# Cross-attention with a gate: score columns laid beside the gate weight, softmax per tile, output shared out over three engines

## The chip, the core and the metric

The kernel runs on one core of one Trainium2 chip. The metric is the device time of one execution in microseconds (us). Before the change it is 416.56 us, the median of three runs. The engines named below are TensorE (PE; its weight loads are listed apart as PEld), VectorE (DVE), ScalarE (ACT), GpSimd (POOL) and SyncE (SP), which here only issues transfers. Each engine runs its own list of instructions in the order written, and engines meet through semaphores: `wait_ge` holds the engine, and all that is written behind it, until a count is reached.

## What is computed

16 batches, 512 queries and 77 keys each, width 512. Cut to what matters, the reference is:

```python
qp = q @ Wq + bq
kp = k @ Wk + bk
vp = v @ Wv + bv
w = jnp.einsum('bqd,bkd->bqk', qp, kp) * scale
w = jax.nn.softmax(w, axis=-1)
x = jnp.einsum('bqk,bkd->bqd', w, vp)
gate = jnp.concatenate((qp, x), axis=-1) @ Wg + bg
x = x * mask[..., None]
x = x * jax.nn.sigmoid(gate)
return x + q0
```

`q0` is the input `q`; keys and values are the same context rows. The mask is one number per row.

## The kernel before

**Precision.** Each product is made of three: an operand is split into a high part (a rounded copy, made by ScalarE) and a low part (what is left, made by VectorE or GpSimd), and high x high, high x low and low x high are summed. So a product over the width of 512 is 4 chunks x 3 = 12 matmuls.

**First stage** (to about 119 us of the trace). Weights are folded: `mt` holds for every batch the 78 key columns (77 and one of zeros) already multiplied by both projections, so that scores are `x @ mt`; `wqg` is the query half of the gate weight multiplied by the query projection; `v_ext` holds per key the value row and beside it that row times the value half of the gate weight. A list of jobs passes through PSUM banks; `v_st` tiles go to memory and come back as `v_ext`.

**Second stage, the loop over 16 batches.** A batch has 4 tiles of 128 queries, numbered n = 4b + t over all batches. `xT` is x turned, with a high and a low part, in two buffers that alternate by batch; its raw form `x_raw` has one buffer. TensorE runs, per batch:

- `gate_main` (L422 to L431): 12 matmuls of 512 columns a tile, `xT` against `wqg`, into one of three banks;
- `turn_probs` (L442): 4 transposes of the probabilities of the whole batch;
- `attend` (L453 to L461): 4 matmuls of 512 columns a tile: two add the value part of the gate to the tile's gate bank, two make the attention output;
- `scores_T` (by the helper at L323): 12 matmuls of 512 columns for the *next* batch, with keys as rows, and `turn_scores` (L401), 4 transposes of them.

ScalarE makes the high part of the next batch's `xT` (L493, four chunks, right at the start of a batch), copies the turned probabilities (L573, L575), and makes the tanh of each tile (L587) and one exp a batch (L497). VectorE does the softmax once a batch in wide instructions (L627 to L634, L724 to L732), the low part of the probabilities (L736) and two instructions a tile: `product` (L744) and `output` (L755), which multiplies by the mask and adds the rows of x. GpSimd makes the low part of `xT` (L781), four chunks in a row, a batch ahead. SyncE's queue loads `x_raw` two batches ahead as soon as it is free, loads the rows and stores the output.

The order around the change is written out by hand, per engine:

```python
for b in range(B):
    more = b + 1 < B
    gate_main(b, 0)
    gate_main(b, 1, range(0, 1))
    turn_probs(b)
    gate_main(b, 1, range(1, C))
    attend(b, 0)
    gate_main(b, 2)
    attend(b, 1)
    if more:
        scores_T(b + 1)
```

## Time and profile before

| | us |
|---|---|
| median of 3 runs (416.47 to 417.1) | 416.56 |
| the profiled execution | 416.89 |
| its span, first to last instruction | 415.1 |
| TensorE busy in it | 407.6 |
| VectorE busy | 228.9 |
| ScalarE busy | 144.7 |
| GpSimd busy | 124.0 |

The span is 1.8 us shorter than the execution's own time. The loop over batches begins at 119.35 us. TensorE matmuls overlap in the records: the length of one is about 0.39 us, while the next one starts 0.23 us after it. So the pace is read from starts, not from lengths.

### The profile page before, as it was taken

The page shows a single profiled execution, that of the slowest core. Times are in us where ns is not written, and L with a number is a line of the kernel's source. Part 1 is how long each engine was busy: PE and PEld are TensorE (multiplying, and loading weights), DVE is VectorE, ACT ScalarE, POOL GpSimd, SP SyncE. Part 2 cuts the span into 40 slices and gives each one's busy share as a digit, 9 for nine tenths or more (in the row PEclk, how much of TensorE's full clock was granted, in tenths as well). Part 3 has the DMA queues.
Part 4 walks back from the last instruction along what each step waited for, and adds up shares of the span by engine and source line. Part 5 has one row for each costly group of instructions (what it writes and reads, how often), then busy time and mean ns, then how long its engine had stood idle before and what let it go on. Part 6 is the DMA issues. An engine that isn't in the chain of part 4 may idle for free.

```text
span 415.1 us, 5234 instructions
## 1 busy us (share of the span) xinstructions
PE 407.6 (98%) x1874; PEld 325.5 (78%) x1874; DVE 228.9 (55%) x404; ACT 144.7 (35%) x251; POOL 124.0 (30%) x96
## 2 busy tenths in 40 slices
PE   8999999999999999999999999999999999999995
PEld 4889986888776878787787878778787877878784
DVE  3687557554563646547364554736455564645554
ACT  5644242325223414233241414424241432324121
POOL 0005125445635405052340505133150504325000
PEclk9999999999999999999999999999999999999999
DMA  7993542568699795866859576786958677595412
GB/s 267 384 415 130 148 130 109 203 200 292 206 305 269 255 304 171 253 196 226 261 189 286 191 252 204 230 221 214 280 199 263 190 242 225 205 275 199 132 53 101
DMA packets 42934, 92.11 MB, mean 222 GB/s; under 512 B 4780, under 2 KB 4780, under 8 KB 42268
## 3 DMA queue, kind: packets, MB, share of 16 engines
q1 hardware_dynamic: 41756, 89.68, 66.4%
q10 hardware_dynamic: 1152, 2.10, 1.6%
q8 instruction: 15, 0.25, 0.3%
q14 instruction: 11, 0.09, 0.1%
HBM read 64.75 MB, written 27.00 MB: 221 GB/s over the span
## 4 chain that ended last, share of the span: by engine, by line
PE 93%; POOL 2%; ACT 2%; DMA 1%; DVE 1%; issue 0%; DVEq 0%
PE bank L430 42%; PE bank L323 32%; PE bank L454 3%; PE bank L461 3%; PE bank L460 3%; PE bank L453 3%; PE bank L346 3%; PE bank L442 2%; POOL xT L781 1%; PE bank L401 1%; DMA wkT_raw<-in_wkT 1%; PE bank L383 1%; POOL wg L781 1%; ACT vT L488 0%; ACT wg L484 0%
## 5 line engine op out<-in xcount | busy, mean ns | idle before, releaser
L430 PE MATMUL bank<-wqg,xT 128*128 128x512 f32 x768 | 192.4, 396 | 0.0
L430 PEld LDWEIGHTS bank<-wqg,xT 128*128 128x128 f32 x768 | 142.1, 188 | 30.6
L781 POOL TENSOR_TENSOR xT<-x_raw,xT 128x512 fp32r<-128x512 f32 x64 | 87.5, 1397 | 178.7 <-ACT xT L493 178.7
L744 DVE SCALAR_TENSOR_TENSOR prod_sb<-tanh_sb,bank 128x512 f32<-128x512 f32 x64 | 43.9, 686 | 72.2 <-ACT tanh_sb L587 72.2
L587 ACT ACTIVATE tanh_sb<-bank 128x512 f32<-128x512 f32 x64 | 38.3, 598 | 125.0 <-PE bank L454 124.3
L755 DVE SCALAR_TENSOR_TENSOR out_sb<-prod_sb,half_mask,x_rows 128x512 f32<-128x512 f32 x64 | 54.5, 851 | 1.7
L323 PE MATMUL bank<-xT,mt 128*77 128x512 f32 x192 | 47.1, 394 | 0.8 <-POOL xT L781 0.8
L323 PEld LDWEIGHTS bank<-xT,mt 128*77 128x77 f32 x192 | 27.8, 146 | 16.9 <-POOL xT L781 1.3
L493 ACT ACTIVATE xT<-x_raw 128x512 fp32r<-128x512 f32 x64 | 35.3, 622 | 0.4 <-DMA x_raw<-in_xT 0.4
L323 PE MATMUL bank<-wv,ctxT 128*128 128x512 f32 (+1 forms) x120 | 30.2, 401 | 0.0
L323 PE MATMUL bank<-wg,vT 128*128 128x512 f32 (+1 forms) x120 | 29.7, 394 | 0.4 <-DVE vT L612 0.3
L736 DVE TENSOR_TENSOR wT<-bank,wT 77x512 fp32r<-77x512 f32 x16 | 11.0, 686 | 30.5 <-ACT wT L573 30.5
L323 PE MATMUL bank<-ctxT,g_s 128*128 128x416 f32 x144 | 27.5, 351 | 0.0
L323 PEld LDWEIGHTS bank<-ctxT,g_s 128*128 128x128 f32 x144 | 26.9, 188 | 0.4
L323 PEld LDWEIGHTS bank<-wg,vT 128*128 128x128 f32 (+1 forms) x120 | 21.9, 185 | 6.4 <-DVE vT L612 0.7
L461 PE MATMUL bank<-v_ext,wT 122*128 122x512 f32 x64 | 25.5, 398 | 0.0
L460 PE MATMUL bank<-v_ext,wT 128*128 128x512 f32 x64 | 25.5, 398 | 0.0
L454 PE MATMUL bank<-v_ext,wT 122*128 122x512 f32 x64 | 25.3, 395 | 0.0
L323 PEld LDWEIGHTS bank<-wv,ctxT 128*128 128x128 f32 (+1 forms) x120 | 21.6, 186 | 4.6
L453 PE MATMUL bank<-v_ext,wT 128*128 128x512 f32 x64 | 25.0, 391 | 0.0
L781 POOL TENSOR_TENSOR v_st<-v_f,v_st 128x512 fp32r<-128x512 f32 (+1 forms) x10 | 13.2, 1316 | 31.4 <-ACT v_st L484 31.4
L627 DVE TENSOR_SCALAR sT<-bank,sb_c 77x512 f32<-77x512 f32 x16 | 11.9, 746 | 18.8 <-PE bank L323 18.8
(73 smaller groups left out, 354.2 us busy)
## 6 DMA issues: line engine op xcount, KB each, us to landing
x_rows<-in_x SPq DMA_DIRECT2D x32, 512.0 KB, 6.9
out_y<-out_sb SPq DMA_DIRECT2D x64, 256.0 KB, 4.3
x_raw<-in_xT SPq DMA_DIRECT2D x60, 256.0 KB, 10.4
v_ext<-v_dram SPq DMA_DIRECT2D x32, 308.0 KB
v_dram<-v_st SPq DMA_DIRECT2D x18, 512.0 KB, 3.3
v_ext<-v_dram SPq DMA_DIRECT2D x16, 180.0 KB
ctxT_raw<-in_ctxT SPq DMA_DIRECT2D x4, 624.0 KB, 10.6
ctx_rows<-in_ctx SPq DMA_DIRECT2D x4, 616.0 KB
```

The source lines that it names most:

```text
L323: last = pe.matmul(ps, lhs(s, c), rhs(m, c), start=(c == 0 and n == 0), stop=(c == C - 1 and n == 2))
L346: last = pe.matmul(bank[bank_of(J["g", cc])][:, :], wkT[:, s, c, cc * P:(cc + 1) * P], wqT[:, m, c, :], start=(c == 0 and n == 0), stop=(c ...
L430: pe.matmul(gate_ps[n % 3][:, :], xT[b % 2][:, s, c, q], wqg[:, m, c, :], start=(c == 0 and (s, m) == PRODUCTS[0]), stop=False)
L453: pe.matmul(ps[:, :], wT[:, 0, q], v[:, 0, D:2 * D], start=False, stop=False)
L454: pe.matmul(ps[:, :], wT[0:K_B, 1, q], v[0:K_B, 1, D:2 * D], start=False, stop=True).then_inc(gate_done, 1)
L460: pe.matmul(ps[:, :], wT[:, 0, q], v[:, 0, 0:D], start=True, stop=False)
L461: pe.matmul(ps[:, :], wT[0:K_B, 1, q], v[0:K_B, 1, 0:D], start=False, stop=True).then_inc(attn_done, 1)
L493: act.activation(xT[b % 2][:, HI, c], x_raw[:, c], ACT.Copy).then_inc(xT_hi, 1)
L587: act.activation(tanh_sb[:, n % 2, :], gate_ps[n % 3][:, :], ACT.Tanh, scale=0.5).then_inc(tanh_made, 1)
L744: dve.scalar_tensor_tensor(prod_sb[:, n % 2, :], tanh_sb[:, n % 2, :], 1.0, attn_ps[n % 2][:, :], ALU.add, ALU.mult).then_inc(prod_made, 1)
L755: dve.scalar_tensor_tensor(out_sb[:, t, :], prod_sb[:, n % 2, :], half_mask[:, n:n + 1], x_rows[b % 2][:, t, :], ALU.mult, ALU.add).then_i ...
L781: pool.tensor_tensor(dst, src, f32(hi_), ALU.subtract).then_inc(made, 1)
```

## The change

The 78 score columns of a batch are laid beside the gate weight in a tile `ws` (two buffers, alternating by batch): two halves, each with 39 score columns, one column of zeros and 256 columns of the gate weight, 296 in all (`HN`). `main` multiplies a tile of x by both halves at once: 24 matmuls of 296 columns a tile, into two PSUM banks. They stand in place of `gate_main`'s 12 of 512 and of `scores_T`'s and `turn_scores`' share. Scores then have queries as rows from the start, and the softmax is done for each tile.

- **ScalarE** copies the gate part out of PSUM (`x_part`), makes the exp with its row sum for a tile, applies the mask (`mask`), makes one chunk of the next batch's `xT` in each tile, and makes the tanh, now from SBUF.
- **VectorE** adds the bias row to the scores, takes maximum, reciprocal and the probabilities for each tile; `gate` adds the value part of the gate, which now has its own PSUM bank, to the copy; `product` stays; `output` goes.
- **GpSimd** adds the rows of x (`output`), copies the score columns of a batch into `ws` (`place_mt`), fills the second `ws` once, and makes one chunk of the low part of `xT` in each tile.
- **SyncE** sends the scores' bias through memory and back as a row for all partitions (`sb_row`).

Core of the diff:

```diff
+            def main(n, chunks):
+                b, q = n // T, slice(n % T * P, (n % T + 1) * P)
+                ps = main_ps[n % 2]
+                if chunks[0] == 0:
+                    pe.wait_ge(xT_lo, (b + 1) * C)
+                    pe.wait_ge(mt_placed, b + 1)
...
+                        pe.wait_ge(gx_made, n - 1)
+                for c in chunks:
+                    for s, m in PRODUCTS:
+                        for h in range(2):
+                            last = pe.matmul(ps[:, h, 0:HN], xT[b % 2][:, s, c, q], ws[b % 2][:, m, c, h, :],
+                                             start=(c == 0 and (s, m) == PRODUCTS[0]), stop=(c == C - 1 and (s, m) == PRODUCTS[2]))
...
+            for n in range(NT + 2):
+                if 0 < n < NT:
+                    main(n, range(0, C // 2))
+                if n >= 2:
+                    attend(n - 2)
+                if n < NT:
+                    main(n, range(C // 2, C - 1))
+                if 1 <= n <= NT:
+                    turn_probs(n - 1)
+                if n < NT:
+                    main(n, range(C - 1, C))
...
+            def x_part(n):
+                act.wait_ge(main_done, n + 1)
+                act.wait_ge(sc_made, n + 1)
...
+                act.activation(gx[:, n % 3, :].rearrange("p (h n) -> p h n", h=2), main_ps[n % 2][:, :, HK + 1:HN], ACT.Copy).then_inc(gx_made, 1)
...
+            for n in range(1, NT + 2):
+                if n <= NT:
+                    x_part(n - 1)
+                    exps(n - 1)
+                if n >= 3:
+                    mask(n - 3)
+                b, c = (n - 1) // T + 1, (n - 1) % T
+                if b < B:
+                    act.wait_ge(main_done, (b - 1) * T)
+                    act.wait_ge(xT_in[c], 16 * (b + 1))
+                    act.activation(xT[b % 2][:, HI, c], x_raw[:, c], ACT.Copy).then_inc(xT_hi, 1)
+                if n >= 2:
+                    tanh_tile(n - 2)
+                if n <= NT:
+                    high_probs(n - 1)
...
+            for n in range(1, NT + 2):
+                if n <= NT:
+                    softmax_max(n - 1)
+                    softmax_rest(n - 1)
+                if n >= 2:
+                    gate(n - 2)
+                if n <= NT:
+                    low_probs(n - 1)
+                if n >= 2:
+                    product(n - 2)
...
+            for n in range(1, NT + 2):
+                b, c = (n - 1) // T + 1, (n - 1) % T
+                if b < B:
+                    xT_lo_of(b, (c,))
+                if c == 0 and 2 <= b < B:
+                    place_mt(b)
+                if n >= 3:
+                    output(n - 3)
```

**TensorE, last tile of batch 0 and first of batch 1.** `psum` is now one tensor of eight banks; `ws_58` and `xT_71` are batch 1's buffers. Before, the same place reads (L442 is `turn_probs` of batch 1):

```order
L430 MATMUL bank<-wqg,xT_68 128x512 x6
L453 MATMUL bank<-v_ext_60,wT 128x512
L454 MATMUL bank<-v_ext_60,wT 128x512
L460 MATMUL bank<-v_ext_60,wT 128x512
L461 MATMUL bank<-v_ext_60,wT 128x512
L430 MATMUL bank<-wqg,xT_69 128x512 x15
L442 MATMUL bank<-ident,prob 128x128 x4
```

and now, with the waits:

```order
L418 MATMUL psum<-ws_57,xT_70 128x296 x6
L430 MATMUL psum<-ident,prob 128x128 [waits wT_lo,prob_made]
L418 MATMUL psum<-ws_57,xT_70 128x296 x6
L418 MATMUL psum<-ws_58,xT_71 128x296 [waits gx_made,mt_placed,xT_lo]
L418 MATMUL psum<-ws_58,xT_71 128x296 x11
L444 MATMUL psum<-v_ext_61,wT 128x512 [waits pre_made,wT_lo,wT_dup]
```

The first matmul of a batch now waits for `xT_lo`, all four chunks of that batch's low part, and `turn_probs` stands in every tile instead of once a batch.

**ScalarE, the same place.** Before, the four chunks of batch 1's `xT` stand together, ahead of all tanh instructions of batch 0:

```order
L493 ACTIVATE xT_69<-x_raw 128x512 [waits xT_in0]
L493 ACTIVATE xT_69<-x_raw 128x512 [waits xT_in1]
L493 ACTIVATE xT_69<-x_raw 128x512 [waits xT_in2]
L493 ACTIVATE xT_69<-x_raw 128x512 [waits xT_in3]
L587 ACTIVATE tanh_sb<-bank 128x512 [waits v_stored1,vg_stored0,vg_stored1,v_stored0,gate_done] x2
```

and now the last chunk of batch 1 stands behind the copy of tile 3's result, which waits for `main_done` of that tile:

```order
L565 ACTIVATE gx<-psum 128x512 [waits tanh_made,sc_made,main_done]
L571 ACTIVATE expd,rowsum<-sc,negmax 128x78 [waits prob_made,negmax_made]
L603 ACTIVATE out_sb<-prod_sb,half_mask 128x512 [waits prod_made]
L615 ACTIVATE xT_71<-x_raw 128x512 [waits xT_in3,main_done]
L594 ACTIVATE tanh_sb<-gx 128x512 [waits prod_made,pre_made]
L581 ACTIVATE wT<-psum 128x128 [waits wT_zeroed,turned]
L583 ACTIVATE wT<-wT 32x128 [waits wT_hi]
```

What moved is the place of the conversion: from a batch ahead to the end of the tile just before its use.

**VectorE, one tile of the loop.** Before, the two instructions of a tile, twice:

```order
L744 SCALAR_TENSOR_TENSOR prod_sb<-tanh_sb,bank 128x512 [waits attn_done,tanh_made]
L755 SCALAR_TENSOR_TENSOR out_sb<-prod_sb,half_mask,x_rows_89 128x512 [waits half_made,x_in00,prod_made]
L744 SCALAR_TENSOR_TENSOR prod_sb<-tanh_sb,bank 128x512 [waits attn_done,tanh_made]
L755 SCALAR_TENSOR_TENSOR out_sb<-prod_sb,half_mask,x_rows_89 128x512 [waits x_in00,prod_made]
L627 TENSOR_SCALAR sT<-bank,sb_c 77x512 [waits sT_done]
```

and now, one tile:

```order
L734 TENSOR_TENSOR sc<-psum,sb_row 128x78 [waits exp_made,main_done]
L736 TENSOR_REDUCE rowmax<-sc 128x1 [waits sc_made]
L738 TENSOR_SCALAR negmax<-rowmax 128x1 [waits max_made]
L743 RECIPROCAL rinv<-rowsum 128x1 [waits exp_made]
L748 TENSOR_SCALAR prob<-expd,rinv 128x77 [waits turned,rinv_made]
L748 TENSOR_SCALAR prob<-expd,rinv 128x19
L748 TENSOR_SCALAR prob<-expd,rinv 128x32
L758 TENSOR_TENSOR gx<-psum,gx 128x512 [waits gx_made,vgate_done]
L753 TENSOR_TENSOR wT<-psum,wT 77x128 [waits wT_hi]
L765 SCALAR_TENSOR_TENSOR prod_sb<-tanh_sb,psum 128x512 [waits attn_done,tanh_made]
```

The wide softmax of four tiles is now ten narrow and wide instructions in each tile, with a wait at nearly every one.

## Rows read from the trace of the kernel before

**Rows 1.** The page: busy time by engine, and the chain that ended last.
```profile
PE 407.6 (98%) x1874; PEld 325.5 (78%) x1874; DVE 228.9 (55%) x404; ACT 144.7 (35%) x251; POOL 124.0 (30%) x96
...
PE 93%; POOL 2%; ACT 2%; DMA 1%; DVE 1%; issue 0%; DVEq 0%
```

**Rows 2.** Timeline of TensorE, one batch: start, length in us, line, operation, tiles, count.
```profile
197.47 0.60 PE L442 MATMUL bank<-ident,prob 128*128 128x128 f32 x4
...
199.99 0.39 PE L453 MATMUL bank<-v_ext,wT 128*128 128x512 f32 x1
...
200.93 2.94 PE L430 MATMUL bank<-wqg,xT 128*128 128x512 f32 x12
...
215.81 0.60 PE L442 MATMUL bank<-ident,prob 128*128 128x128 f32 x4
```

**Rows 3.** Timeline: shorter matmuls, two weight loads in a row, the first matmuls.
```profile
44.71 2.61 PE L323 MATMUL bank<-ctxT,g_s 128*128 128x416 f32 x13
...
6.22 0.30 PEld L346 LDWEIGHTS bank<-wqT,wkT 128*128 128x128 f32 x2 [1.49 <-ACT wkT L484]
...
1.19 4.44 PE L337 MATMUL bank<-zeros 128*128 128x512 bf16 x10 [1.19 <-DVE zeros L644]
```

**Rows 4.** Groups by line and form (busy us, mean ns, idle before); last two: minimum/median/maximum ns.
```profile
L781 POOL TENSOR_TENSOR xT<-x_raw,xT 128x512 fp32r<-128x512 f32 x64 | 87.5, 1397 | 178.7 <-ACT xT L493 178.7
...
L744 DVE SCALAR_TENSOR_TENSOR prod_sb<-tanh_sb,bank 128x512 f32<-128x512 f32 x64 | 43.9, 686 | 72.2 <-ACT tanh_sb L587 72.2
L587 ACT ACTIVATE tanh_sb<-bank 128x512 f32<-128x512 f32 x64 | 38.3, 598 | 125.0 <-PE bank L454 124.3 <-DMA v_dram<-v_st 0.8
L493 ACT ACTIVATE xT<-x_raw 128x512 fp32r<-128x512 f32 x64 | 35.3, 622 | 0.4 <-DMA x_raw<-in_xT 0.4
...
L573 ACT ACTIVATE wT<-bank 128x512 fp32r<-128x512 f32 x16 | 9.6, 599 | 29.1 <-PE bank L442 29.1
...
L724 DVE TENSOR_REDUCE rowsum<-expd 128x4 f32<-128x308 f32 x16 | 7.5, 467 | 0.0
L497 ACT ACTIVATE expd<-shifted 128x308 f32<-128x308 f32 x16 | 7.4, 463 | 42.4 <-DVE shifted L634 42.4
...
L726 DVE RECIPROCAL rinv<-rowsum 128x4 f32<-128x4 f32 x16 | 2.9, 178 | 0.5
...
L685 DVE TENSOR_SCALAR half_mask<-mask_c 128x64 f32<-128x64 f32 x1 | 0.2, 188 | 0.0
...
L731 DVE TENSOR_TENSOR prob<-expd,rinv x16: 229/230/1324, 121.4 to 396.1; 128x76 f32<-128x76 f32 x16
L732 DVE TENSOR_TENSOR prob<-expd,rinv x16: 278/284/285, 122.6 to 396.2; 128x128 f32<-128x128 f32 x16
```

**Rows 5.** Timeline: hops from engine to engine, ScalarE to GpSimd among them.
```profile
124.93 2.19 ACT L493 ACTIVATE xT<-x_raw 128x512 fp32r<-128x512 f32 x4
...
125.64 5.48 POOL L781 TENSOR_TENSOR xT<-x_raw,xT 128x512 fp32r<-128x512 f32 x4 [3.06 <-ACT xT L493]
```

**Rows 6.** VectorE's output instruction alone: minimum/median/maximum ns.
```profile
L755 DVE SCALAR_TENSOR_TENSOR out_sb<-prod_sb,half_mask,x_rows x64: 741/752/1679, 129.2 to 411.8; 128x512 f32<-128x512 f32 x64
```

**Rows 7.** Timeline where the loop begins, and the landing time of a row sent to all partitions.
```profile
119.35 3.56 PE L430 MATMUL bank<-wqg,xT 128*128 128x512 f32 x15
...
121.08 1.51 POOL L781 TENSOR_TENSOR v_st<-vg_f,v_st 96x512 fp32r<-96x512 f32 x1 [4.88 <-ACT v_st L484]
...
DMA to landing us min/median/max: 5.1/5.1/5.1
```

**Rows 8.** Timeline of the end; then stretches: busy us by engine, PEclk (granted clock), DMA.
```profile
410.52 0.40 PE L461 MATMUL bank<-v_ext,wT 122*128 122x512 f32 x1
...
412.62 0.33 SPq L312 DMA_DIRECT2D out_y<-out_sb  x1
...
5.48:411.00 405.52, 403.27 (x1865) 324.12 (x1864) 227.17 (x401) 142.83 (x250) 123.27 (x90) 1.00 0.69 224
...
415.08:415.10 0.02, 0.00 (x0) 0.00 (x0) 0.00 (x0) 0.00 (x0) 0.00 (x0) 0.50 0.00 0
```

More of the change, by code:

```diff
@@ L24 @@
 KROWS = [min(P, KEYS - k * P) for k in range(KT)]
+HK = SP // 2
+HN = HK + 1 + D // 2
+OUT_OF_SIGHT = -1e30
 MB = 3
@@ new lines, in turn_probs, with attend @@
+            def turn_probs(n):
+                pe.wait_ge(prob_made, 3 * (n + 1))
+                if n == 0:
+                    pe.wait_ge(job_drained, last_in_bank(7))
+                else:
+                    pe.wait_ge(wT_lo, n)
+                t = n % T
+                pe.transpose(turn_ps[:, t * P:(t + 1) * P], prob[:, n % 2, :], ident[:, :]).then_inc(turned, 1)
+            def attend(n):
+                b, q = n // T, slice(n % T * P, (n % T + 1) * P)
+                v = v_ext[b % 2]
+                pe.wait_ge(wT_dup, n + 1)
+                pe.wait_ge(wT_lo, n + 1)
+                if n % T == 0:
+                    pe.wait_ge(vext_in[b % 2], 80 * (b // 2 + 1))
+                if n >= 2:
+                    pe.wait_ge(pre_made, n - 1)
+                else:
+                    pe.wait_ge(job_drained, last_in_bank(2 + n))
+                ps = vgate_ps[n % 2]
+                pe.matmul(ps[:, :], wT[:, 0, q], v[:, 0, D:2 * D], start=True, stop=False)
+                pe.matmul(ps[:, :], wT[0:K_B, 1, q], v[0:K_B, 1, D:2 * D], start=False, stop=True).then_inc(vgate_done, 1)
+                if n:
+                    pe.wait_ge(prod_made, n)
+                else:
+                    pe.wait_ge(job_drained, last_in_bank(6))
+                pe.matmul(attn_ps[:, :], wT[:, 0, q], v[:, 0, 0:D], start=True, stop=False)
+                pe.matmul(attn_ps[:, :], wT[0:K_B, 1, q], v[0:K_B, 1, 0:D], start=False, stop=True).then_inc(attn_done, 1)
@@ L408, in _ @@
                 else:
-                    scores_T(0)
+                    main(0, range(0, C // 2))
                 n = KROWS[k - 1]
@@ L433, in turn_probs @@
-            def turn_probs(b):
-                pe.wait_ge(prob_made, b + 1)
-                pe.wait_ge(prob_twice, 2 * (b + 1))
-                if b == 0:
-                    pe.wait_ge(job_drained, last_in_bank(7))
-                else:
-                    pe.wait_ge(wTb_made, b)
-                    pe.wait_ge(wT_lo, b)
-                for t in range(T):
-                    last = pe.transpose(turn_ps[:, t * P:(t + 1) * P], prob[:, t, :], ident[:, :])
-                last.then_inc(turned, 1)
@@ new lines, in softmax_rest @@
+            def softmax_rest(n):
+                i, t = n % 2, slice(n % T, n % T + 1)
+                dve.wait_ge(exp_made, n + 1)
+                dve.reciprocal(rinv[:, t], rowsum[:, t]).then_inc(rinv_made, 1)
+                dve.wait_ge(rinv_made, n + 1)
+                if n >= 2:
+                    dve.wait_ge(turned, n - 1)
+                for to, at in ((slice(0, S), slice(0, S)), (slice(S, TOP), slice(DUP, S)), (slice(TOP, P), slice(0, Q))):
+                    dve.tensor_scalar(prob[:, i, to], expd[:, i, at], rinv[:, t], None, ALU.mult).then_inc(prob_made, 1)
@@ new lines, in low_probs, with gate, product @@
+            def low_probs(n):
+                q = slice(n % T * P, (n % T + 1) * P)
+                dve.wait_ge(wT_hi, n + 1)
+                dve.tensor_tensor(wT[0:S, 1, q], turn_ps[0:S, q], f32(wT[0:S, 0, q]), ALU.subtract).then_inc(wT_lo, 1)
+            def gate(n):
+                dve.wait_ge(vgate_done, n + 1)
+                dve.wait_ge(gx_made, n + 1)
+                dve.tensor_tensor(gx[:, n % 3, :], vgate_ps[n % 2][:, :], gx[:, n % 3, :], ALU.add).then_inc(pre_made, 1)
+            def product(n):
```

282 lines of the change are left out of this document (110 added, 172 removed).

## The prediction, made before the changed kernel was run

> **What bounds the kernel now.** The page first: TensorE is busy 98% of the span, and 93% of the chain that ended last is TensorE [rows 1]. The other engines' idle time costs nothing. The timeline then gives the pace. One batch takes 215.81 − 197.47 = 18.34 us. Twelve matmuls of 512 columns take (2.94 − 0.396) / 11 = 0.231 us each from start to start, the four of `attend` 0.94 us together, and a transpose (0.60 − 0.272) / 3 = 0.11 us [rows 2]. A change gains what it takes off that row of matmuls, and only while nobody makes TensorE wait. Today nobody does, because everything it needs is made a batch ahead: GpSimd gets four chunks of `xT` in a row, long before their use [rows 5].
>
> **TensorE's own work.** Per tile it had 12 matmuls for the gate and 3 for the scores; now it has 24 of 296 columns. Matmuls of 416 columns start (2.61 − 0.351) / 12 = 0.188 us apart [rows 3], those of 512, 0.231. The line through both gives 0.135 us at 296: 7104 columns a tile instead of 7680, but nine more fixed shares. A tile is 24 × 0.135 + 0.94 + 0.11 = 4.29 us against 18.34 / 4 = 4.59: 0.30 us less, 19 us over 64 tiles, if TensorE never waits. The line holds only if weight loads keep up. A single load lasts 0.188 us, just the spacing of the 416 column matmuls; but two loads in a row take 0.30 us together [rows 3], so they can start 0.11 us apart. I take 0.135, with 0.188 as the upper end.
>
> The Trainium skill (TensorE: Matmul & The Clock Gate, section LDWEIGHTS) prices a load of 128 columns at 128 / 1.2 = 107 ns whatever the rows; the trace agrees with 0.11. By it, loads stay hidden behind 296 columns.
>
> **The loop between VectorE and ScalarE.** Each now has one list per tile, in which every step waits for the one before, and the lists cross twice. Let VectorE's addition of the score bias for a tile start at 0.
> - Addition, maximum and scaling: 0.23 each for 76 columns, taken for the first two, and 0.16, with three hops of 0.04: 0.73. Meanwhile ScalarE copies the gate part, 0.04 + 0.60 after the addition, to 0.87; so exp starts at 0.90. By the slope from 308 to 512 columns (463 to 622 ns) it takes 0.29: 1.19.
> - Reciprocal 0.08 + 0.18, three probability instructions 0.56 or a little less (0.188 for 64 columns): 2.0.
> - `gate`, 0.69 with one input in PSUM, as `product`: 2.72. Tanh 0.63: 3.35. High part of the turned probabilities, 128 columns, 0.60 less 384 columns at 0.78 ns: 0.30 + 0.03: 3.68. Low part 0.28 + 0.03: 3.99. `product` 0.69 + 0.04: 4.72. Next addition: **4.75 us** [rows 4].
>
> ScalarE's other work of a tile (mask 0.62, one chunk of `xT` 0.62) fits between 1.2 and 2.5, and GpSimd's two instructions are 2 × 1.4, so neither is the limit. TensorE, at 4.29, is not either: it stands about 0.5 us a tile at `turn_probs`. So the loop already runs slower than the 4.59 of before: the 0.30 won is given back and 0.16 more. Bounds: 4.4 (shorter small instructions, TensorE then sets the pace) and 5.1 (a slow write of the row sum, not shown in this trace; fresh hops of 0.08).
>
> **The start of each batch.** The last chunk of the next batch's `xT` now stands on ScalarE behind the gate copy and exp of the batch's last tile, and the copy waits for that tile's last matmul. TensorE's very next instruction is the new batch's first matmul, which waits for that chunk's low part. Nothing lies between, so it is all exposed. On the same clock: exp done 1.19, mask 1.84, high part 2.49, hop to GpSimd 0.09 [rows 5] and 1.40 for the low part: 3.98; TensorE starts at 4.04. Queued behind it are `attend` of the tile two back, the transposes of the last tile, and through them all of VectorE's gate work. Twelve matmuls 1.62, `attend` 0.94, six matmuls 0.81: transposes at 7.41, result 0.30 later; high part 8.05, low part 8.36, `product` 9.09, next addition at **9.13** instead of 4.75. TensorE is idle about 5.5 us at each of 15 places. Bounds: 8.7 and 9.9. A batch is 3 × 4.75 + 9.13 = 23.4 us against 18.34.
>
> **Start and end.** The bias row goes to memory and back behind the last store of the first stage, which waits for GpSimd's low part (121.08 + 1.51, some 0.6 earlier now, as 12 short matmuls replace 12 long ones): 122.0, issue 0.5, landing 5.1 for a row of 512 sent to all partitions [rows 7], this one 2.4 times as long and behind stores: about 128. TensorE, which began its loop at 119.35, waits there for the first probabilities until 130. From this the additions of tiles 1, 2 and 3 start at 131.2, 136.1 and 140.9. GpSimd's filling of the second `ws` (4096 elements a partition, bounded by 2.7 ns each, the pace of its subtraction, 11 us) is covered by this and by three tiles; if its end slipped, the first new batch would bear it.
>
> The end was: last attention matmul at 410.52, end of span at 415.1, 4.6 us [rows 8]. Now after the last addition: probabilities 2.03, turned 2.43, high part behind the tanh of the tile before 3.68, low part 3.99, gate matmuls 4.68, `gate` 5.45, tanh 6.08, `product` 6.8, mask 7.45, rows on GpSimd 8.94, store 2.5 (the last from 412.62 to the end): 11.4.
>
> **VectorE and GpSimd together.** `output` took 0.75 us, but up to 1.68 [rows 6], and the 76 column instruction 0.23 and once 1.32 [rows 4]; both read SBUF alone. Where one of these meets GpSimd at work it seems to wait for its end. In the new order GpSimd is idle when the probabilities are made, except in the tile with the copy of score columns: 0.3 × 14 = 4 us, from 0 to 7.
>
> The Trainium skill (SBUF — State Buffer, section Who interferes with whom) says that VectorE's two-port forms, `tensor_scalar` among them, and GpSimd block each other fully. By it every probability instruction could be held for a GpSimd one; that is rival four.
>
> **The clock.** It was granted in full through the loop, 1.00 of 2.4 GHz, and was at 0.50 (1.2 GHz) only at 415.08, 4.6 us after the last matmul's start [rows 8]. At the low clock 512 column matmuls start (4.44 − 0.63) / 9 = 0.42 us apart [rows 3]. No idle time of 5.5 us is in the trace with matmuls behind it. I take it that the clock falls at about 8 of 15 places and costs 2 us each (some 4 us at little over half pace, as after the first matmul at 1.19): 16 us, from 0 to 30.
>
> The Trainium skill (the same TensorE page, section Why this matters for your kernels) warns against idle gaps between bursts of matmuls, since the clock drops to half; by it the higher end is the likelier.
>
> **Sum.** 140.9 + 45 × 4.75 + 15 × 9.13 + 4 + 11.4 = 507.0; with the clock 523.0; the profiled execution is 1.8 over its span (416.89 to 415.1), 524.8; it lies 0.3 over the median: **524.5 us**.
>
> **Rivals.**
> 1. *The loop is hidden, the batch starts are not.* If small instructions are shorter, TensorE sets the pace: 4.4 a tile, 8.8 at a batch start: 140.9 + 198 + 132 + 2 + 11 + 1.5 = 485, with some clock 492. For it: the margin is only 0.4 us. 12%.
> 2. *Weight loads bind.* Spacing 0.188: TensorE needs 5.55 a tile, 10.1 at a batch start: 143 + 250 + 152 + 11 + 2 = 558, with clock 572. For it: the 416 column row alone. Against it: two loads 0.11 apart. 7%.
> 3. *Faster.* The columns are what counts, and the batch start is covered: 64 × 0.30 = 19 us off, 7 back at the start of the loop, 7 at the end: 412 us. This decides if a batch start costs TensorE under 0.3 us. It needs the last chunk to be ready when the last tile's matmuls end; the order puts it behind an instruction that waits for that end. 2%.
> 4. *VectorE and GpSimd block each other* in most tiles, 0.7 us a tile more: 524 + 45 = 569. Against it: by the schedule above they don't meet. 7%.
> 5. *The change doesn't do what it says*: the score matmuls stay beside the new ones. The order of the changed kernel rules it out: no matmul with 77 rows of keys is left. No share.
>
> **How the numbers follow.** My case 72%. Its own range: 4.5 to 5.0 a tile (−11, +11), 8.8 to 9.7 at a batch start (−5, +9), clock 0 to 30 (−16, +14): some 495 to 550. Rival 1 pulls the low end to 478; half of rivals 2 and 4 are taken in by 565. A measurement of this kernel can tell about 0.2%, 0.8 us, from no change. Faster 2%, the same 1%, slower 97%.
>
> **What would show it.** TensorE's matmul line at 296 columns with starts 0.135 apart (0.19: rival 2). Its busy share near 65 to 75%. In the list of waits, TensorE's main line waits for GpSimd's `xT` 15 times at 5 to 6 us; `turn_probs` waits for VectorE about 0.5 us a tile, once 7 us at the first. A batch every 23 us, in the chain ScalarE and VectorE where TensorE stood. PEclk with low slices. Wrong would make it: a batch near 18 us, transposes that never wait, or small instructions of over 0.3 us.

## The result, and the profile after

The changed kernel takes 519.77 us (median of 4 runs, 518.61 to 520.48), the kernel before on the same chip 416.82 us. The ratio is 1.247, with a 95% interval of 1.244 to 1.250: slower by 103 us. The span of the profiled execution is 516.8 us, that of before 415.1.

The page of the changed kernel, busy time by engine, the granted clock in forty slices, and three groups:

```profile
PE 422.2 (82%) x2386; PEld 384.7 (74%) x2386; DVE 251.1 (49%) x773; ACT 258.2 (50%) x587; POOL 213.2 (41%) x180
...
PEclk9999999999679797989899898989898989989897
...
issue 41%; POOL 32%; PE 19%; DMA 3%; ACT 1%; DVE 1%; SPq 1%; POOLq 0%; ACTq 0%; DVEq 0%
...
L418 PE MATMUL psum<-ws,xT 128*128 128x296 f32 x1536 | 251.5, 321 | 71.4 <-POOL xT L785 71.4
...
L748 DVE TENSOR_SCALAR prob<-expd,rinv 128x77 f32<-128x77 f32 (+2 forms) x192 | 35.2, 242 | 2.2
```

Against [rows 1], TensorE has fallen from 98% to 82% of the span, and the chain that ended last has lost it: 19% instead of 93%. No other engine is near its limit (49, 50, 41%). No engine is full and the kernel is slower: that points to engines that wait for each other. The chain runs along GpSimd's instructions, and 41% of it is "issue", time for which the profile shows no releaser, so it settles little; the list of waits tells more.

```profile
POOL xT L785 <- ACT xT L615: 201.7, 60, 8.6
ACT tanh_sb L594 <- DVE gx L758: 108.7, 64, 6.3
DVE gx L758 <- PE psum L445: 87.1, 17, 6.0
...
PE psum L418 <- POOL xT L785: 71.4, 15, 5.0
...
PE psum L430 <- DVE prob L748: 12.0, 2, 10.6
```

(us in total, times, longest.) TensorE stands 15 times, once at each new batch, for GpSimd's low part of `xT`, 4.8 us each (71.4 / 15). The timeline of one such place:

```profile
218.35 0.27 DVE L734 TENSOR_TENSOR sc<-psum,sb_row 128x78 f32<-128x78 f32 x1
...
219.68 0.71 ACT L603 ACTIVATE out_sb<-prod_sb,half_mask 128x512 f32<-128x512 f32 x1
...
220.29 0.61 ACT L615 ACTIVATE xT<-x_raw 128x512 fp32r<-128x512 f32 x1
220.98 1.26 POOL L785 TENSOR_TENSOR xT<-x_raw,xT 128x512 fp32r<-128x512 f32 x1 [1.95 <-ACT xT L615]
...
222.30 3.03 PE L418 MATMUL psum<-ws,xT 128*128 128x296 f32 x12 [4.71 <-POOL xT L785]
...
226.50 0.98 PE L418 MATMUL psum<-ws,xT 128*128 128x296 f32 x6
...
228.74 0.27 DVE L734 TENSOR_TENSOR sc<-psum,sb_row 128x78 f32<-128x78 f32 x1
```

TensorE starts 3.95 us after the last addition of the score bias (218.35), close to the forecast 4.04, and the next addition comes 10.39 us after it. Twelve matmuls take 3.03 us here; six take 0.98 us a moment later. The difference is the clock, which is granted at its lower level in most of the second stretch below (length, busy us by engine, PEclk, DMA share and GB/s):

```profile
201.00:222.20 21.20, 16.59 (x107) 15.53 (x105) 11.19 (x40) 13.27 (x32) 9.46 (x8) 0.97 0.56 176
222.20:225.70 3.50, 3.40 (x14) 3.31 (x15) 0.00 (x0) 0.00 (x0) 1.27 (x2) 0.57 0.62 167
```

The additions give the whole time. The 48 steps within a batch are 4.48 us (median; 45 of them are within 0.05 of it), the 15 steps into a new batch 10.53 on average. Counted against four tiles of 18.34 / 4 = 4.585 us [rows 2]:

- 64 tiles at 4.48 instead of 4.585: −7 us
- 15 × (10.53 − 4.48): +91 us, of which 24 are the clock (shown below) and 67 the wait itself
- what is left of the difference of the spans, 101.7 us: +18 us, at the head (the last 30 matmuls ahead of the first transposes start at 118.56, and the first addition comes at 131.26, since it waits for the bias row) and at the tail (last addition 505.06 to 516.8)

```profile
118.56 4.27 PE L418 MATMUL psum<-ws,xT 128*128 128x296 f32 x30
133.41 0.48 PE L430 MATMUL psum<-ident,prob 128*128 128x128 f32 x1 [10.58 <-DVE prob L748]
```

### The profile page after: what moved, and what is told of

The parts are those of the page before. It is cut to its first block, busy times and chain, and to the rows that moved or that the text cites. A ratio compares the mean times of both kernels' runs of the same rounds, so it can differ in the third digit from the quotient of the medians.

```text
span 516.8 us, 7632 instructions
## 1 busy us (share of the span) xinstructions
PE 422.2 (82%) x2386; PEld 384.7 (74%) x2386; DVE 251.1 (49%) x773; ACT 258.2 (50%) x587; POOL 213.2 (41%) x180
## 4 chain that ended last, share of the span: by engine, by line
issue 41%; POOL 32%; PE 19%; DMA 3%; ACT 1%; DVE 1%; SPq 1%; POOLq 0%; ACTq 0%; DVEq 0%
PE psum L339 16%; POOL out_sb L842 15%; POOL xT L785 14%; PE psum L362 2%; DMA sb_dram<-sb_c 2%; POOL ws L796 2%; DMA wkT_raw<-in_wkT 1%; DMA sb_row<-sb_dram 1%; POOL wg L785 1%; PE psum L399 1%; PE psum L418 0%; POOLq L85 0%; ACT vT L487 0%; POOLq L841 0%; ACT wg L483 0%
## 5 line engine op out<-in xcount | busy, mean ns | idle before, releaser
L418 PE MATMUL psum<-ws,xT 128*128 128x296 f32 x1536 | 251.5, 321 | 71.4 <-POOL xT L785 71.4
L418 PEld LDWEIGHTS psum<-ws,xT 128*128 128x128 f32 x1536 | 237.3, 204 | 80.7 <-POOL xT L785 75.0
L594 ACT ACTIVATE tanh_sb<-gx 128x512 f32<-128x512 f32 x64 | 40.5, 632 | 108.7 <-DVE gx L758 108.7
L842 POOL TENSOR_TENSOR out_sb<-out_sb,x_rows 128x512 f32<-128x512 f32 x64 | 82.1, 1283 | 20.2 <-ACT out_sb L603 20.2
L758 DVE TENSOR_TENSOR gx<-psum,gx 128x512 f32<-128x512 f32 x64 | 43.9, 685 | 87.1 <-PE psum L445 87.1
L565 ACT ACTIVATE gx<-psum 128x512 f32<-128x512 f32 x64 | 38.3, 599 | 66.1 <-DVE sc L734 66.1
L603 ACT ACTIVATE out_sb<-prod_sb,half_mask 128x512 f32<-128x512 f32 x64 | 45.3, 708 | 1.4 <-DVE prod_sb L765 1.4
L765 DVE SCALAR_TENSOR_TENSOR prod_sb<-tanh_sb,psum 128x512 f32<-128x512 f32 x64 | 43.1, 674 | 0.9 <-ACT tanh_sb L594 0.7
L748 DVE TENSOR_SCALAR prob<-expd,rinv 128x77 f32<-128x77 f32 (+2 forms) x192 | 35.2, 242 | 2.2
L444 PE MATMUL psum<-v_ext,wT 128*128 128x512 f32 x64 | 28.9, 452 | 1.8 <-ACT wT L583 1.8
L450 PE MATMUL psum<-v_ext,wT 128*128 128x512 f32 x64 | 26.6, 415 | 0.0
```

The source lines that it names most:

```text
L418: last = pe.matmul(ps[:, h, 0:HN], xT[b % 2][:, s, c, q], ws[b % 2][:, m, c, h, :], start=(c == 0 and (s, m) == PRODUCTS[0]), stop=(c == C ...
L444: pe.matmul(ps[:, :], wT[:, 0, q], v[:, 0, D:2 * D], start=True, stop=False)
L565: act.activation(gx[:, n % 3, :].rearrange("p (h n) -> p h n", h=2), main_ps[n % 2][:, :, HK + 1:HN], ACT.Copy).then_inc(gx_made, 1)
L594: act.activation(tanh_sb[:, n % 2, :], gx[:, n % 3, :], ACT.Tanh, scale=0.5).then_inc(tanh_made, 1)
L603: act.activation(out_sb[:, t, :], prod_sb[:, n % 2, :], ACT.Copy, scale=half_mask[:, n:n + 1]).then_inc(masked, 1)
L748: dve.tensor_scalar(prob[:, i, to], expd[:, i, at], rinv[:, t], None, ALU.mult).then_inc(prob_made, 1)
```

## The experiments

All compute what the changed kernel does. "Step" is the time from one tile's score addition to the next; t0 to t3 are a batch's tiles, and the step into a new batch is the one from t3 to t0. An instruction is called held when it takes over 0.65 us instead of about 0.23.

**1. The price of the clock alone.** Short matmuls, `WARM` = 38 of 128 columns, fill TensorE's wait at a batch start; their sums are overwritten.

```diff
+                if chunks[0] == 0 and n % T == 0 and n:
+                    pe.wait_ge(wT_lo, n - 1)
+                    for _ in range(WARM):
+                        pe.matmul(turn_ps[:, 3 * P:4 * P], xT[(b - 1) % 2][:, HI, 0, 3 * P:4 * P], ws[(b - 1) % 2][:, HI, 0, 0, 0:P],
+                                  start=True, stop=True)
                 if chunks[0] == 0:
                     pe.wait_ge(xT_lo, (b + 1) * C)
```

> The changed kernel, with 38 extra matmuls of 128 columns on TensorE in the gap at each batch start (their result is overwritten), so that the array is not idle; the wait for xT_lo stays. My theory (the fallen clock costs 12 matmuls 1.2 us and attend 0.4 us each time, all on the path): PEclk 1.00 through the loop after the first tiles, the step at a batch start 8.9 instead of 10.5 us; 520 - 15 x 1.6 = 496 us. Rival (the low clock lies beside the work of VectorE and ScalarE and costs nothing): within 1 us of 520. If the extra matmuls run past the moment at which xT is ready, the gain is smaller: 38 x 0.11 = 4.1 us against a gap of 5.0 less 0.8.

Measured: 495.66 us, ratio 1.188 (1.184 to 1.192). Between 140.7 and 480 us the granted clock is 1.00, and the step into a new batch falls from 10.53 to 8.93, the rest staying 4.48:

```profile
140.70:480.00 339.30, 334.16 (x2339) 318.11 (x2338) 170.14 (x606) 200.17 (x483) 158.39 (x132) 1.00 0.55 177
```

So the low clock costs 24 us in the steps, 1.6 at each of 15 places; TensorE still starts its batch 4.0 us after the last addition, as before, and the other 67 us are that wait. Busy is no progress here: TensorE is busy 98% of this stretch, since the throwaway matmuls count, and the kernel is still 19% slower than before.

**2. Whose instructions set the step.** The output goes back to VectorE as one instruction; ScalarE's mask and GpSimd's sum are gone.

```diff
                     product(n - 2)
+                    output(n - 2)
...
-                    mask(n - 3)
...
-                    output(n - 3)
```

> The changed kernel with the output made as before, by one VectorE instruction behind product; ScalarE's mask and GpSimd's sum are gone. My theory (VectorE and ScalarE form one chain round the tile, 4.48 us): VectorE's 0.75 us and a hop of 0.04 enter the chain: 5.27 us a tile, the step at a batch start about the same (0.71 less before the conversion, 0.79 more in the chain), the end 1.3 us shorter; 520 + 48 x 0.79 + 1 - 1 = 558 us. Rival (VectorE is busy 49% only, so its idle time takes the instruction in): 515 to 522 us.

Measured: 568.44 us, 1.364 (1.360 to 1.368). The step within a batch is 5.26 us (median of 48; 46 are within 0.05 of it), as expected; the timeline shows the 0.75 us instruction standing in the row:

```profile
223.26 0.67 DVE L762 SCALAR_TENSOR_TENSOR prod_sb<-tanh_sb,psum 128x512 f32<-128x512 f32 x1
223.97 0.75 DVE L773 SCALAR_TENSOR_TENSOR out_sb<-prod_sb,half_mask,x_rows 128x512 f32<-128x512 f32 x1
224.63 0.27 DVE L731 TENSOR_TENSOR sc<-psum,sb_row 128x78 f32<-128x78 f32 x1
```

VectorE is far from full, yet this instruction lengthened the step by its whole length: the loop between the engines is the bound. Sharing the output over three engines is thus a useful part of the change. The total missed by 10 us: the step into a new batch took 11.49 on average, not 10.6. TensorE stood 5.2 us each time instead of 4.8, and the low clock then lasted 6.8 us at all 15 places; in the changed kernel it lasted 3.4 us at 12 of them and 6.8 at the first three. That the longer wait is what kept it low for longer is not shown: those first three followed waits of 4.4 to 4.8 us.

**3. The head.** The score bias is sent and read back on ScalarE's queue.

```diff
-            sync.wait_ge(sb_made, 1)
-            sync.dma_start(sb_dram, sb_c[:, :]).then_inc(sb_out, 16)
...
+                if k == KT:
+                    act.wait_ge(sb_made, 1)
+                    act.dma_start(sb_dram, sb_c[:, :]).then_inc(sb_out, 16)
+                    act.wait_ge(sb_out, 16)
```

> The changed kernel with the two transfers of the score bias moved from SyncE's queue to ScalarE's, ahead of its last v_st copy. My theory (TensorE's 10.9 us of waiting at its first transpose is these two transfers behind the stores): the first addition of VectorE starts at about 122 instead of 131.3, the first wait of TensorE falls to about 2 us; 520 - 9 = 511 us. Rival (the transfers themselves take that long, whatever the queue): no more than 3 us gained, 517 or more.

Measured: 517.21 us, 1.241 (1.238 to 1.245), 2.6 us less than the changed kernel. The rival held. The bias was sent at 115.0 instead of 117.1, but the read-back could only follow at 122.4 and took 6.7 us instead of 3.7:

```profile
114.98 0.57 ACTq L550 DMA_DIRECT2D sb_dram<-sb_c  x1
122.40 0.36 ACTq L552 DMA_DIRECT2D sb_row<-sb_dram  x1
```

The transfers, not SyncE's queue, are what takes the time here.

**4. The next batch's `xT` a tile earlier.** ScalarE and GpSimd convert two quarters in a batch's first tile, none in the last.

```diff
+CHUNKS = [(0, 1), (2,), (3,), ()]
-                b, c = (n - 1) // T + 1, (n - 1) % T
-                if b < B:
+                b = (n - 1) // T + 1
+                for c in CHUNKS[(n - 1) % T]:
```

> Only the place of the conversion of xT is changed against the changed kernel: ScalarE and GpSimd make chunks 0 and 1 in the first tile of a batch, 2 in the second, 3 in the third, none in the fourth, so the last low part is ready a tile before TensorE asks for it. My theory (the batch start costs what lies between gx of the last tile and the low part of chunk 3): the step at a batch start falls from 10.5 us to about 4.5, the tile with two chunks grows by 0.1 to 0.3, no wait of TensorE for GpSimd's xT is left, the clock stays at 1.00 in the loop; 520 - 15 x 6.0 + 3 = 432 us. Rival (something else is late at a batch start too: the x_raw transfers or GpSimd's queue): a wait of 1 us or more stays at each, 447 us or more.

Measured: 481.83 us, 1.157 (1.151 to 1.163); the step into a new batch is 4.5, but the next one, t0 to t1, is 7.40 on average and the one behind it 4.91. TensorE's wait for `xT` went from 71.4 to 5.8 us, and another took its place:

```profile
ACT xT L617 <- DMA x_raw<-in_xT: 39.2, 13, 4.1
...
PE psum L445 <- ACT wT L584: 26.2, 15, 2.9
```

ScalarE now waits for `x_raw`, and so the turned probabilities, which it copies behind the conversion, reach TensorE late. `x_raw` has one buffer. It is refilled after all four quarters are read, and behind the five `v_ext` transfers in SyncE's queue: too late for a use a tile earlier.

**5. The same, with each quarter refilled as soon as it is read.**

```diff
-                if b + 2 < B:
-                    sync.wait_ge(xT_lo, (b + 2) * C)
-                    load_xT(b + 2)
...
+                for c in CHUNKS[(n - 1) % T]:
+                    if b + 1 < B:
+                        sync.wait_ge(xT_lo, b * C + c + 1)
+                        load_xT(b + 1, (c,))
```

> e1_early with one thing more: SyncE loads each chunk of x_raw again as soon as its low part is made, in place of all four behind the third chunk and behind the five v_ext transfers of the next batch. My theory (what was late in e1_early is the x_raw transfer, issued 7 us before its use and landing after 10): the step at a batch start falls from 7.4 to about 4.5 us, ScalarE's wait for x_raw (39 us in all in e1_early) goes, no low clock in the loop; e1_early's 482 less 15 x 2.9 and 15 x 0.4 = 432 us. Rival (the DMA engines are full, so transfers are late whenever issued): 460 us or more, with ScalarE still waiting for x_raw.

Measured: 453.94 us, 1.091 (1.086 to 1.095), between the two theories. The wait for `x_raw` is gone, the step into a batch is 4.5, but t1 to t2 is 5.96: `v_ext` now lands late.

```profile
PE psum L448 <- DMA v_ext<-v_dram: 20.4, 12, 2.4
```

Fourteen probability instructions also took 0.84 to 0.89 us instead of 0.23. In the changed kernel none does.

**6. A shorter row on ScalarE: exp ahead of the gate copy,** and the conversion of `xT` behind the turned probabilities (the second move is not in the cut below). Both are added to experiment 5.

```diff
-                    x_part(n - 1)
                     exps(n - 1)
+                    x_part(n - 1)
```

> e6_chunk_loads with ScalarE's order in a tile changed: exp ahead of the copy of the gate part, and the conversion of xT behind the turned probabilities. My theory (4.48 us a tile is the chain VectorE - ScalarE - VectorE, in which the copy of 0.6 us stands between the addition and exp): the chain falls by 0.27 us to 4.21, and TensorE's own 4.33 us becomes the bound; 60 x 0.15 = 9 us less than e6_chunk_loads, 423 us. Rival (the tile is bound by something else, as TensorE already): the same as e6_chunk_loads within 2 us.

Measured: 530.2 us, 1.274 (1.272 to 1.276), where 423 was expected. The step t0 to t1 did become 4.32, TensorE's own. The others are 6.8, 5.2 and 8.3 on average. The timeline shows why:

```profile
330.36 0.55 DVE L753 TENSOR_SCALAR prob<-expd,rinv 128x77 f32<-128x77 f32 x3
333.46 2.54 POOL L790 TENSOR_TENSOR xT<-x_raw,xT 128x512 fp32r<-128x512 f32 x2 [9.70 <-ACT xT L624]
334.68 3.23 DVE L753 TENSOR_SCALAR prob<-expd,rinv 128x77 f32<-128x77 f32 x3
...
PE psum L434 <- DVE prob L753: 44.2, 30, 10.5
PE psum L422 <- POOL xT L790: 38.4, 15, 2.6
```

Three instructions take 0.55 us with GpSimd idle and 3.23 us beside it. TensorE then waits for the probabilities, and also for the last low part of `xT`, since its conversion now comes later (44 and 38 us in all). 87 of 192 take 0.7 to 1.4 us, and each of these has a GpSimd instruction over its whole length: rival 4 of the prediction, in a kernel whose order lets the two meet.

**7. Experiment 6 with the bias also sent a round earlier.**

```diff
-                if k == KT - 1:
+                if k == KT - 2:
                     dve.wait_ge(dots_made, DOT["sb", SB_ORDER[-1]] + 1)
```

> e7_exp_first with the score bias sent to memory one job round earlier (about 108 us instead of 117) and read back ahead of v_ext. In e4_sb_act each of the two transfers took about 7 us to land, so only an earlier start helps. My theory: VectorE's first addition at 121 instead of 131 us, TensorE's first wait under 2 us, no low clock but at the end; 10 us less than e7_exp_first, about 412 us, 1% faster than the kernel before. Rival (GpSimd's filling of the second ws, which ends at 127 us, now holds batch 1): 3 to 5 us of the 10 come back as a wait of TensorE for xT at the first batch start.

Measured: 523.94 us, 1.259 (1.257 to 1.261). The first addition comes at 123.1 instead of 131.5, and 6.3 of these 8.4 us arrive in the total. The loop is that of experiment 6.

**8. Is it the form of the instruction?** The probabilities of experiment 6 as `tensor_tensor`, reading the same two tiles in SBUF.

```diff
-                    dve.tensor_scalar(prob[:, i, to], expd[:, i, at], rinv[:, t], None, ALU.mult).then_inc(prob_made, 1)
+                    dve.tensor_tensor(prob[:, i, to], expd[:, i, at], rinv[:, t].broadcast_to([P, to.stop - to.start]), ALU.mult).then_inc(prob_made, 1)
```

> e7_exp_first with one edit: the three probability instructions of a tile are tensor_tensor products with the reciprocal column broadcast, as in the kernel before, in place of tensor_scalar products. Work, order and waits are otherwise those of e7_exp_first (530.2 us). Theory A, a tensor_scalar of fp32 cannot run beside a GpSimd instruction and is held until that instruction has ended (0.70 and 1.28 to 1.50 us instead of 0.23 in e7_exp_first, always with a GpSimd instruction over its whole length), while a tensor_tensor, such as the gate's addition, is not: none of the 192 instructions is over 0.35 us, tiles step 4.32 us, TensorE's speed, throughout but for up to 0.7 us a batch on late v_ext transfers, 16 x 17.3 + 16 x 0.7 = 288 from the first addition at 131.5, end 12 later: 432 us. Rival B, a form makes no difference, and what holds VectorE is the SBUF traffic of GpSimd itself, or the wait for the turned probabilities of two tiles back: tensor_tensor is stretched as well, and the time stays over 510 us.

Measured: 504.58 us, 1.213 (1.206 to 1.220). My theory fell in this form: 55 instructions still take 0.73 to 1.28 us. The rival did not hold whole either, for the form does make a difference: 87 held instructions became 55, and the time fell by 26 us. The trace has 61 more of them beside GpSimd's work that take 0.18 to 0.24 us. Each of these starts within 0.05 us of the start of a GpSimd instruction; in experiment 6 86 of the 87 started as close (within 0.06 us) and were held.

```profile
332.12 1.52 DVE L753 TENSOR_TENSOR prob<-expd,rinv 128x77 f32<-128x77 f32 x3
332.13 2.65 POOL L847 TENSOR_TENSOR out_sb<-out_sb,x_rows 128x512 f32<-128x512 f32 x2
```

**9. The same with the bias, `v_ext` and placement moved.**

```diff
+                b, t = (n - 2) // T, (n - 2) % T
+                if t == 0 and 1 <= b < B - 1:
+                    sync.wait_ge(attn_done, b * T)
+                    load_vext(b + 1)
...
-                if c == 0 and 2 <= b < B:
+                if c == 3 and 2 <= b < B:
                     place_mt(b)
```

> e8_prob_tt with the score bias sent a round earlier (as in e5_all, first addition at 123.1), the v_ext transfers of the next batch issued one tile earlier, as soon as the batch that read that buffer is attended, and GpSimd's placing of the score columns moved from a batch's first tile, where it stands beside two low parts and an output (about 6.3 us of GpSimd in one tile of 4.3), to its last tile, where no low part stands. Theory A: 8.4 us earlier at the start, no waits for v_ext, all tiles at 4.32: 123.1 + 63 x 4.32 + 12 + 1.8 = 409 us, below the kernel before (416.8). Rival: the transfers still land late in the tile of the batch change or GpSimd's two low parts make xT late, 0.7 to 1 us a batch: 420 to 424 us. If the form of the probabilities makes no difference: over 505.

Measured: 529.12 us, 1.274 (1.269 to 1.279). 52 instructions are held, and one move was a mistake: on GpSimd the score columns now stand behind the low part and the output of the tile before, and that low part waits for ScalarE's conversion, which experiment 6 had moved to the end of its row. TensorE starts 0.1 us after the columns are placed; it stood 4.6 us at 14 of 15 batch starts (the profile shows no releaser for this wait), and their steps are 10.6 us long:

```profile
316.30 1.26 POOL L791 TENSOR_TENSOR xT<-x_raw,xT 128x512 fp32r<-128x512 f32 x1 [2.64 <-ACT xT L625]
317.52 1.35 POOL L848 TENSOR_TENSOR out_sb<-out_sb,x_rows 128x512 f32<-128x512 f32 x1
318.82 0.70 POOL L802 CAST ws<-mt 128x624 fp32r<-128x624 f32 x1
...
319.62 2.81 PE L423 MATMUL psum<-ws,xT 128*128 128x296 f32 x10 [4.61 <-issue]
```

**10. Or what the instruction reads?** Experiment 6 with the exponentials in a PSUM bank; the probability instruction is `tensor_scalar` again, with one input from PSUM. For this the value part of the gate gives up one of its two banks.

```diff
-                act.activation(expd[:, n % 2, :], sc[:, n % 2, :, :].rearrange("p h k -> p (h k)"), ACT.Exp, bias=negmax[:, n % T:n % T + 1],
+                act.activation(exp_ps[:, 0:SP], sc[:, n % 2, :, :].rearrange("p h k -> p (h k)"), ACT.Exp, bias=negmax[:, n % T:n % T + 1],
...
-                    dve.tensor_scalar(prob[:, i, to], expd[:, i, at], rinv[:, t], None, ALU.mult).then_inc(prob_made, 1)
+                    dve.tensor_scalar(prob[:, i, to], exp_ps[:, at], rinv[:, t], None, ALU.mult).then_inc(prob_made, 1)
```

> e7_exp_first with one change: the exponentials are written to a PSUM bank (the one freed by giving the gate's value part one bank instead of two), so that each probability instruction reads one operand from PSUM and writes SBUF. In e8_prob_tt the tensor_tensor form was held as the tensor_scalar form had been (84 of 192 instructions over 0.7 us, all under a GpSimd instruction), while the score addition, the gate's addition and the product, which each read one operand from PSUM and one from SBUF, never were. Theory A, VectorE is held only by instructions with two SBUF inputs or a doubled rate from SBUF: no probability instruction is over 0.35 us. Tiles then step 4.3 to 4.6 within a batch; the tile of the batch change keeps TensorE's 2.9 us wait for the last low part and 1.6 us of low clock, 8.0 to 8.9: batch 21.5, 131.5 + 15 x 21.5 + 13 + 12 + 1.8 = 481 us (475 to 492). Rival B, GpSimd stretches whatever VectorE does in that place in the program: instructions of 0.7 and 1.3 us remain, over 500 us.

(The 84 held instructions that this text gives for experiment 8 are 55 by the trace.) Measured: 479.37 us, 1.151 (1.147 to 1.154), as theory A had it (481). No instruction of 192 is over 0.302 us, in the same order, and 132 of them have GpSimd at work beside them for at least 90% of their length:

```profile
L755 DVE TENSOR_SCALAR prob<-psum,rinv x192: 226/243/302, 133.0 to 468.1; 128x77 f32<-128x77 f32 x64, 128x19 f32<-128x19 f32 x64, 128x32 f32<-128x32 f32 x64
...
328.95 2.53 POOL L792 TENSOR_TENSOR xT<-x_raw,xT 128x512 fp32r<-128x512 f32 x2 [7.12 <-ACT xT L626]
330.17 0.60 DVE L755 TENSOR_SCALAR prob<-psum,rinv 128x77 f32<-128x77 f32 x3
...
PE psum L422 <- POOL xT L792: 28.3, 15, 2.0
```

That is worth 51 us against experiment 6, with one operand moved. What decides whether VectorE is held is where its inputs lie. It is still 25 us more than experiment 5: the conversion of `xT`, behind the turned probabilities, is late again, and TensorE stands 1.9 us for it at each of 15 batch starts (last line), where experiment 5 had 1.5 us in all.

**11. All of it together:** experiment 9's moves with the exponentials in PSUM, the placement in a batch's third tile (the cut is against experiment 9), and the conversion back behind the mask.

```diff
-                if c == 3 and 2 <= b < B:
+                if c == 2 and 2 <= b < B:
                     place_mt(b)
```

> Exponentials in PSUM as in e12_exp_psum, and ScalarE's conversions of xT in the place behind the mask (as in e1_early and e6_chunk_loads, not behind the turned probabilities), score bias a round earlier, v_ext transfers a tile earlier, GpSimd's placing of the score columns in a batch's third tile. Theory A: nothing holds VectorE, xT is ready a tile ahead, TensorE is never idle for over 0.5 us after 135 us and the clock does not fall: 123.1 + 63 x 4.32 + 12 + 1.8 = 409 us, under the kernel before (416.3). Rival: the double conversion on ScalarE in a batch's first tile (about 1.2 us more in its chain) or the transfers cost 0.5 to 1 us a batch: 417 to 425. If instructions are still held by GpSimd: over 440.

Measured: 447.23 us, 1.074 (1.069 to 1.078), 38 more than theory A. No instruction is held, but steps are 4.96, 4.45, 4.45 and mostly 5.5 to 7: the double conversion lengthens ScalarE's row in a batch's first tile (with one, in experiment 12, that step is 4.60), and TensorE still stands 1.7 us for the last quarter at 14 batch starts:

```profile
PE psum L423 <- POOL xT L793: 23.4, 14, 1.7
```

The earlier bias did little (tile 2's addition came at 139.1 instead of 141.0), since TensorE then stood 4.1 us for the first `v_ext`.

**12. A wait per quarter of `xT`, one conversion a tile,** both against experiment 11.

```diff
-CHUNKS = [(0, 1), (2,), (3,), ()]
+CHUNKS = [(0,), (1,), (2,), (3,)]
...
-                    pe.wait_ge(xT_lo, (b + 1) * C)
...
                 for c in chunks:
+                    pe.wait_ge(xT_lo, b * C + c + 1)
```

> e11_all_psum (447.2 us) with two edits: TensorE waits for the low part of each quarter of xT just ahead of the first products that read it, in place of waiting for all four ahead of a batch, and ScalarE and GpSimd convert one quarter per tile again (in e11_all_psum two in a batch's first tile). In e11_all_psum a batch takes 4.96 + 4.45 + 4.45 + 5.5 = 19.3 us: 0.5 for the double conversion on ScalarE, 0.7 to 1.0 for the last quarter. Theory A, no wait of over 0.4 us is left and ScalarE's and VectorE's chain sets 4.45 for every tile: a batch of 17.8 to 18.1, from the third addition at 139.1: 139.1 + 61 x 4.45 + 15 x 0.2 + 12 + 1.8 = 427 us (424 to 432), still above the kernel before, whose tile in the same loop is TensorE's. Rival: the last quarter, converted behind the mask of the batch's own last tile, comes later than its products by more than 1 us and the batch stays at 19 us: 440 or more.

Measured: 440.42 us, 1.057 (1.055 to 1.059), the best of these, and still slower than the kernel before. Steps are 4.60, 4.45, 4.45 and 5.48. The number is the rival's, its reason is not: the wait is now for the placing of the score columns, behind a low part on GpSimd.

```profile
PE psum L423 <- POOL ws L804: 15.8, 14, 1.2
```

Even with that gone (15 × (5.48 − 4.45)) it would be about 425 us, an estimate from these steps. No version that beats the kernel before was found.

## Why the prediction was right

The sign, the mechanism and the size held: 524.5 forecast, 519.8 measured. The span was forecast as 523.0 and came out 6.2 shorter. By its steps:

- **TensorE's own work.** Starts are 0.137 us apart at 296 columns (median; forecast 0.135), so loads don't bind and rival 2 is out. A tile that nothing holds up took 4.32 us (forecast 4.29), in experiments 6, 8 and 10 from addition to addition, and in the changed kernel from transpose to transpose (lines below).
- **The loop between VectorE and ScalarE** was mis-sized: 4.48, not 4.75, −12 us over 45 steps. That it binds was right: experiment 2 adds one VectorE instruction of 0.75 and the step grows by 0.78. The error lies in its second half. Tanh starts 2.85 us after the addition, 0.13 later than forecast (exp and its row sum, which has a record of its own, 0.19 us, took longer), but from there to the next addition it is 1.63 instead of 2.03:

```profile
228.74 0.27 DVE L734 TENSOR_TENSOR sc<-psum,sb_row 128x78 f32<-128x78 f32 x1
...
231.59 0.63 ACT L594 ACTIVATE tanh_sb<-gx 128x512 f32<-128x512 f32 x1 [0.27 <-DVE gx L758]
232.12 0.26 ACT L581 ACTIVATE wT<-psum 128x128 fp32r<-128x128 f32 x1
...
232.41 0.29 DVE L753 TENSOR_TENSOR wT<-psum,wT 77x128 fp32r<-77x128 f32 x1 [0.86 <-ACT wT L581]
232.62 0.67 DVE L765 SCALAR_TENSOR_TENSOR prod_sb<-tanh_sb,psum 128x512 f32<-128x512 f32 x1
233.22 0.28 DVE L734 TENSOR_TENSOR sc<-psum,sb_row 128x78 f32<-128x78 f32 x1
```

  Behind tanh, behind the low part and behind `product`, the next instruction of the same engine starts 0.07 to 0.10 us before the recorded end of the one ahead. I had added whole lengths and a hop each time.
- **TensorE inside a batch** was wrong: it was to stand about 0.5 us a tile at `turn_probs`. Its only waits there are at the first tile of all (10.6 us) and at the last (1.4 us). Inside a batch it runs at its own 4.33 us and gets ahead of the additions, and it gives this back in the one wait at the batch's end. The time of a batch is set by the additions all the same, since the last conversion hangs on them. Rival 1's margin was thus 4.48 − 4.32 = 0.16 us, less than the 0.4 it was given.

```profile
227.32 0.27 PE L430 MATMUL psum<-ident,prob 128*128 128x128 f32 x1
...
231.65 0.27 PE L430 MATMUL psum<-ident,prob 128*128 128x128 f32 x1
```

- **The start of each batch**: 8.93 at full clock, in experiment 1, against 9.13. TensorE stood 4.8 us each, forecast 5.5. Experiment 4 shows that it is the place of the conversion: with the conversion a tile earlier the step into a batch is 4.5.
- **The clock**: mis-sized the other way. It fell at all 15 places, not 8, and cost 1.6 us each, not 2: 24 instead of 16 us. The Trainium skill (TensorE: Matmul & The Clock Gate, section Why this matters for your kernels) had made the higher end likelier; the granted clock, low after each of the 15 waits (0.57 in the stretch shown), agrees.
- **Start and end.** Tile 3's addition came 4.5 us later than forecast (145.44 for 140.9). About 3 of these are the bias row: its read-back was issued only at 127.40 and landed at 131.1, not 128. The rest fell in the next tiles; the granted clock was 0.50 from 127.2 to 137.3, after TensorE's wait of 10.6 us, a fall that the forecast had not counted. The end took 11.7 instead of 11.4.
- **VectorE and GpSimd together**: nothing, against 4 us. The forecast that they hardly meet in this order was right: no probability instruction is over 0.267 us, and only 8 of 192 touch a GpSimd instruction at all. Only by that is rival 4 out. How narrow that was, experiment 6 shows: it moved two instructions on ScalarE, 87 probability instructions were held, and the kernel took 530 us. That the order kept them apart was more luck than margin.

−12 (tile), −4 (collisions), −3 (batch start), +8 (clock), +4.5 and +0.3 (start, end) make −6. So the total is closer than its terms, which missed by up to 12 us, some one way and some the other.

Rival 3 needed a covered batch start; experiments 4, 5, 11 and 12 come nearer to it step by step (482, 454, 447, 440) and show the price of each cover: a raw tile refilled in time, `v_ext`, ScalarE's row. "The change doesn't do what it says" was rightly given nothing.

## What to carry to other kernels

A batched softmax that is pulled into every tile puts two engines in a loop; then the sum of lengths around the loop counts, not how busy anyone is, and each helper of the next batch belongs in the list where its user is a tile away, not next in line. When a producer is moved earlier, follow its inputs back (buffer, queue, transfer) before pricing the gain. And before moving an instruction of VectorE or GpSimd in time, see what the other one does there and whether one input of VectorE's instruction can lie in PSUM.

## What the runs showed of the hardware

- A VectorE instruction that reads SBUF alone, a `tensor_scalar` from SBUF to SBUF or a `tensor_tensor` with both inputs there, can be held until GpSimd's instruction has ended: 0.23 us become 0.7 to 1.4. With one input in PSUM it never was (0 of 192 in experiment 10, 132 of them beside a GpSimd instruction). The Trainium skill (SBUF — State Buffer, section Who interferes with whom) states both cases, two inputs and the two-port forms; the prediction had taken only the second from it, and experiment 8 paid for the first. The held rows agree. The kernel before shows it too, in an output instruction that reads two tiles in SBUF: median 0.752, up to 1.679 us [rows 6]; 14 of 64 take over 1.1 us, each with GpSimd at work beside it.
- The two forms differ when both engines start together. Of the `tensor_scalar` instructions of experiment 6 that lay beside a GpSimd one all 87 were held, 86 of them started within 0.06 us of its start; of the `tensor_tensor` instructions of experiment 8 61 started as close and ran in 0.18 to 0.24 us. Why is not shown.
- TensorE's waits of 4.8 us on average were each followed by at least 3.4 us at half clock, at three of 15 places by 6.8 us; in experiment 2, with waits of 5.2 us, it was 6.8 us at all 15, and the step into a batch was 0.9 us longer than expected.
- The same read-back of the bias row took 3.7 us after the stores (issued at 127.4) and 6.7 us among them (at 122.4, experiment 3).
